# A fused transformer block on one core: a table-load trigger removed, the second feed-forward product and the fusing product in 64-column tiles, its result copied by ScalarE and turned back

## The reference

```python
item, geo, visit = emb[ids], geo_table[ids], visit_table[ids]     # 64, 64, 24 wide
cat   = [gelu(item @ w_item + b), gelu(geo @ w_geo + b), gelu(visit @ w_visit + b)]
fused = layer_norm(gelu(cat @ w_fuse + b_fuse)) * gamma + beta    # exact gelu
h     = item + 0.1 * fused * (ids != 0)
# attention, 4 heads of 16, over 128 tokens of a sequence, on layernorm(h)
h     = h + (softmax(q k^T / 4) v).bf16 @ Wo.T + bo
x3    = layernorm(h)
y     = gelu_tanh(x3 @ w1 + b1) @ w2 + b2                         # 64 -> 256 -> 64
# 63 tokens of each sequence with the largest router weight r = x3 @ wr + br get r * y
out   = h + x3 + where(chosen, r * y, 0)
```

## Time and profile before

| | us |
|---|---|
| median of 3 runs | 574.9 |
| lowest, highest | 573.29, 576.59 |
| the profiled execution, whole | 569.05 |
| its span, first to last instruction | 567.2 |
| PE busy (share of the span) | 463.9 (82%) |
| DVE busy | 434.5 (77%) |
| ACT busy | 376.1 (66%) |
| POOL busy | 344.9 (61%) |
| table loads at L419, L451, L466 | 38.5, 39.8, 41.1 |

### The profile page before, as it was taken

The page is one execution under the profiler, slowest core; times in us unless marked ns, Lnnn a source line. Parts: engine busy times, 40 slices in busy tenths (PEclk is TensorE's granted clock), DMA queues, the critical chain, the costliest instruction groups (busy, mean ns, idle before and its releaser), DMA issues.

```text
span 567.2 us, 16166 instructions
## 1 busy us (share of the span) xinstructions
PE 463.9 (82%) x5636; PEld 362.8 (64%) x5636; DVE 434.5 (77%) x1657; ACT 376.1 (66%) x662; POOL 344.9 (61%) x410
## 2 busy tenths in 40 slices
PE   0677688888899888888888889888888888876853
PEld 0455566666677766676666777776667666665643
DVE  1366677887878878787878888887877887877787
ACT  0425577777777777777777787777777777755540
POOL 5466366765675756666666676666666666431464
PEclk9979899999999999999999999999999999989555
DMA  4112111111110111111111111111111111000244
GB/s 101 22 25 31 15 25 24 24 25 23 17 20 13 20 20 23 23 23 23 23 23 22 20 17 19 17 18 23 23 23 23 23 23 23 1 2 3 70 114 113
DMA packets 23716, 15.80 MB, mean 28 GB/s; under 512 B 18832, under 2 KB 21520, under 8 KB 23568
## 3 DMA queue, kind: packets, MB, share of 16 engines
q0 software_dynamic: 6144, 9.97, 12.3%
q1 hardware_dynamic: 17552, 5.58, 3.7%
HBM read 11.08 MB, written 4.19 MB: 27 GB/s over the span
## 4 chain that ended last, share of the span: by engine, by line
PE 31%; issue 25%; DVE 19%; POOL 11%; ACT 11%; DVEq 1%; DMA 1%; ACTq 0%; POOLq 0%
POOL G L306 5%; ACT prob L466 5%; PE psum L865 4%; PE psum L953 4%; POOL rs L314 4%; PE psum L917 3%; DVE neg_max L614 3%; PE psum L873 3%; PE psum L943 3%; PE psum L810 3%; DVE st L509 3%; PE psum L894 2%; ACT hid L459 2%; DVE mv L516 2%; DVE s L531 2%
## 5 line engine op out<-in xcount | busy, mean ns | idle before, releaser
L314 POOL TENSOR_TENSOR rs<-ve,minus_half 128x4 f32<-128x4 f32 x96 | 101.0, 1052 | 133.3 <-DVE ve L519 128.6
L306 POOL DMA_INDIRECT G<-table,idx x128 | 125.2, 978 | 40.3 <-issue 36.6
L614 DVE TENSOR_REDUCE neg_max<-psum 128x4 f32<-128x512 f32 x128 | 84.4, 682 | 3.9 <-PE psum L865 3.9
L953 PE MATMUL psum<-x3t,wt 64*128 64x256 f32 x256 | 38.3, 420 | 41.9 <-issue 34.9
L459 ACT ACTIVATE hid<-psum,wt 128x512 f32<-128x512 f32 x64 | 40.5, 683 | 45.4 <-PE psum L953 45.4
L786 PE MATMUL psum<-wt,hid 128*128 128x64 f32 x512 | 68.8, 291 | 0.0
L466 ACT ACTIVATE prob<-psum 128x512 f32<-128x512 f32 x128 | 66.1, 603 | 2.0 <-PE psum L828 1.7
L786 PEld LDWEIGHTS psum<-wt,hid 128*128 128x128 f32 x512 | 64.5, 205 | 3.8 <-issue 0.4
L953 PEld LDWEIGHTS psum<-x3t,wt 64*128 64x128 f32 x256 | 23.0, 194 | 50.9 <-issue 41.1
L865 PE MATMUL psum<-k_s,q_s 32*128 32x128 f32 x1024 | 39.3, 292 | 12.5 <-ACT prob L466 12.4
L509 DVE BATCH_NORM_STATS2 st<-psum 128x6 f32<-128x64 f32 x128 | 20.0, 219 | 35.4 <-PE psum L943 30.5
(11 more groups left out here) (113 smaller groups left out, 1084.3 us busy)
## 6 DMA issues: line engine op xcount, KB each, us to landing
out<-R SPq DMA_DIRECT2D x11, 256.0 KB, 2.9
G<-table,idx POOLq DMA_INDIRECT x128
wt<-packed SPq DMA_DIRECT2D x1, 1028.0 KB, 4.9
out<-R SPq DMA_DIRECT2D x2, 512.0 KB, 4.1
q_s<-max_t SPq DMA_DIRECT2D x32, 8.0 KB
out<-R SPq DMA_DIRECT2D x2, 128.0 KB, 2.6
ids_sb<-ids SPq DMA_DIRECT2D x1, 64.0 KB, 1.8
```

Of the source, the lines that this page charges most:

```text
L306: pool.indirect_dma_start(G[par][:, b, :], None, table, bass.IndirectOffsetOnAxis(ap=idx[par][:, b:b + 1], axis=0),).then_inc(gathered[par ...
L314: pool.tensor_tensor(rs[:, :], ve[:, :], minus_half[:, :], ALU.pow).then_inc(S[dst], 1)
L614: dve.tensor_reduce(neg_max[:, GB * h:GB * h + GB], bank[h].rearrange("p (b k) -> p b k", b=GB), AX, ALU.max, negate=True).then_inc(S["max ...
L953: mm(bank[ffn_bank(d) + r][:, m * 2 * P:(m + 1) * 2 * P], w["w_1"][rows, m * P:(m + 1) * P], x3t[rows, :], start=True, stop=True, tile_pos ...
```

## The change

- ACT: the one-element activation (L451) is gone. The x3t copy comes at once after q_s, and the load of the tanh-gelu table stands ahead of the first hid activation.
- PE: the second feed-forward product is turned round. w_2 (64 columns a half) is the stationary side and hid the moving one, four products of 256 columns, two of them at a time in the two column halves of the array. The result comes out with features on partitions, so a new ACT copy (`ffn_copy`, with the bias b_2 added) takes it to SBUF (`y_t`) and two new PE transposes (`ffn_back`) turn it back into PSUM. `ffn_out` on DVE becomes a plain copy. The ACT copy stands between the first and the second exponential, the transposes behind the output projection.
- PE: the fusing product uses one 64-column weight, w_f, in the two column halves for even and odd sequences, in place of two padded weights.
- One weight of 128 columns and the broadcast b2 leave the packed constants.

```diff
-    ("w_ig", P), ("w_vi", 2 * P), ("w_fe", P), ("w_fo", P), ("w_fv", P), ("w_2", 2 * D),
+    ("w_ig", P), ("w_vi", 2 * P), ("w_f", D), ("w_fv", P), ("w_2", 2 * D),
...
+            def ffn_copy(d):
+                wait(act, "f2_ready", 1, d)
+                ends(act, "yb_ready", 1, d - 1)
+                act.activation(y_t[:, :], bank[ffn_bank(d) + 1][:, 0:2 * P], ACT.Identity,
+                               bias=w["b_2"]).then_inc(S["yt_ready"], 1)
...
                 if on(d):
-                    act.activation(loaded[:, :], w["b_q"][0:1, :], ACT.Gelu_apprx_tanh)
                     wait(act, "x3t_ready", 1, d)
                     act.activation(x3t[:, :], bank[ffn_bank(d) + 1][:, 0:2 * P], ACT.Copy
                                    ).then_inc(S["x3t_out"], 1)
+                if type(i) is int and i == NG + 1:
+                    ffn_copy(NG - 2)
...
                                        ACT.Exp, scale=SCALE).then_inc(S["prob_ready"], 1)
+                    if h == 0 and on(d) and not late(i):
+                        ffn_copy(d)
...
             def ffn_out(d):
-                wait(dve, "f2_ready", 1, d)
-                dve.tensor_tensor(
-                    of(Y, d), bank[ffn_bank(d) + 1][:, 0:GB * D].rearrange("p (b d) -> p b d", b=GB),
-                    w["b2"].unsqueeze(1).to_broadcast([P, GB, D]), ALU.add
+                wait(dve, "yb_ready", 1, d)
+                dve.tensor_copy(
+                    of(Y, d), bank[ffn_bank(d) + 1][:, 0:GB * D].rearrange("p (b d) -> p b d", b=GB)
...
             def ffn_second(d):
                 wait(pe, "hid_ready", 2, d)
-                for s in range(GB):
-                    for m in range(2):
-                        last = mm(bank[ffn_bank(d) + 1][:, s * D:(s + 1) * D],
-                                  hid[:, m, slot(s)[0]], w["w_2"][:, m * D:(m + 1) * D],
-                                  start=(m == 0), stop=(m == 1))
+                for m in range(2):
+                    for r in range(2):
+                        last = mm(bank[ffn_bank(d) + 1][r * D:(r + 1) * D, 0:2 * P],
+                                  w["w_2"][:, m * D:(m + 1) * D],
+                                  hid[:, m, r * 2 * P:(r + 1) * 2 * P],
+                                  start=(m == 0), stop=(m == 1), tile_position=(0, r * D))
                 last.then_inc(S["f2_ready"], 1)
+            def ffn_back(d):
+                wait(pe, "yt_ready", 1, d)
+                for j in range(2):
+                    last = mm(bank[ffn_bank(d) + 1][:, j * P:(j + 1) * P],
+                              y_t[:, j * P:(j + 1) * P], ident, start=True, stop=True,
+                              is_transpose=True)
+                last.then_inc(S["yb_ready"], 1)
...
-                    for n, wf in enumerate(("w_fe", "w_fo")):
-                        last = mm(bank[6][:, 0:2 * P], w[wf],
+                    for n in range(2):
+                        last = mm(bank[6][n * D:(n + 1) * D, 0:2 * P], w["w_f"],
                                   cat[:, :].rearrange("p (r s q) -> p s r q", r=2, s=2)[:, n],
-                                  start=False, stop=(n == 1))
+                                  start=False, stop=True, tile_position=(0, n * D))
...
                 if type(i) is int and i == NG + 1:
                     ffn_second(NG - 2)
+                    ffn_back(NG - 2)
...
                 if on(e) and not late(i):
                     project(e)
+                if on(d) and not late(i):
+                    ffn_back(d)
             pipeline(pe, step)
             coefficients(1)
             ffn_second(NG - 1)
+            ffn_back(NG - 1)
```

More of the change, by code:

```diff
@@ L67 @@
     ("w_q", P), ("w_k", P), ("w_v", P), ("w_1", HID),
-    ("w_ig", P), ("w_vi", 2 * P), ("w_fe", P), ("w_fo", P), ("w_fv", P), ("w_2", 2 * D),
+    ("w_ig", P), ("w_vi", 2 * P), ("w_f", D), ("w_fv", P), ("w_2", 2 * D),
     ("w_o", D), ("ident", P),
-    ("gamma", D), ("beta", D), ("bv", D), ("b2", D), ("wr", D), ("br", 1),
-    ("b_ig", 1), ("b_vi", 1), ("b_fu", 1), ("b_q", 1), ("b_k", 1), ("b_1", 2),
+    ("gamma", D), ("beta", D), ("bv", D), ("wr", D), ("br", 1),
+    ("b_ig", 1), ("b_vi", 1), ("b_fu", 1), ("b_q", 1), ("b_k", 1), ("b_1", 2), ("b_2", 1),
 ]
@@ L144, in build @@
         hid = sb("hid", [P, 2, GT])
-        loaded = sb("loaded", [1, 1])
+        y_t = sb("y_t", [P, 2 * P])
         wt_rank = sb("wt_rank", [P, P])
@@ L179, in build @@
             "xw_ready", "w_ready", "r_ready", "x3t_ready", "x3t_out", "f1_ready",
-            "hid_ready", "f2_ready", "y_ready",
+            "hid_ready", "f2_ready", "yt_ready", "yb_ready", "y_ready",
         )}
@@ L468, in step @@
                                        ACT.Exp, scale=SCALE).then_inc(S["prob_ready"], 1)
+                    if h == 0 and on(d) and not late(i):
+                        ffn_copy(d)
             pipeline(act, step)
+            ffn_copy(NG - 1)
         @block.vector
@@ L1009 @@
     wf = np.asarray(L0_tok_w_fuse)
-    c["w_fe"][:, :D] = c["w_fo"][:, D:] = wf[:P]
+    c["w_f"][:] = wf[:P]
     c["w_fv"][:D, :D] = c["w_fv"][D:, D:] = wf[P:]
@@ L1015 @@
     for n, src in (("gamma", L0_tok_ln_gamma), ("beta", L0_tok_ln_beta), ("bv", L0_attn_bv),
-                   ("b2", L0_ffn_b2), ("wr", L0_ffn_wr), ("br", L0_ffn_br)):
+                   ("wr", L0_ffn_wr), ("br", L0_ffn_br)):
         c[n][:] = np.asarray(src).reshape(1, -1)
     c["b_ig"][:D, 0], c["b_ig"][D:, 0] = np.asarray(L0_tok_b_item), np.asarray(L0_tok_b_geo)
-    for n, src in (("b_vi", L0_tok_b_visit), ("b_fu", L0_tok_b_fuse)):
+    for n, src in (("b_vi", L0_tok_b_visit), ("b_fu", L0_tok_b_fuse), ("b_2", L0_ffn_b2)):
         c[n][:D, 0] = c[n][D:, 0] = np.asarray(src)
```

## The result

| | before | changed |
|---|---|---|
| median of 9 runs each, us | 574.7 | 583.8 |
| lowest, highest | 569.49, 576.59 | 576.7, 587.28 |
| the profiled execution | 569.05 | 581.16 |

What follows compares the result with a forecast made beforehand. Two alternating wait loops bound it: ACT/PE (15.25 to 14.2 us: -1.27 + 0.4 - 0.2) and DVE (14.56, then ruling). Saving 0.86 over 26 steps, 22.4 - 2.5 + 0.4, about 20 us off 574.9 gave 555; range 547 to 569.

Steps and rivals of the forecast that it cites:

- The two loops: Waits bounding steps 4 to 29 in turn: one through ACT and PE, 15.25 us a step; one through DVE, 14.56.
- the term for the trigger: ACT in the loop: removing L451 puts the table load under the first feed-forward product; hid starts 1.27 us earlier.
- the written-out steps: Steps 2, 3, 30 and later: table load and first feed-forward product stay sequential; gain 0 to 0.2 us each, taken as 0.
- the first loop: Through ACT and PE, from first feed-forward product via hid and exponentials back: 15.25 us a step before, 14.2 forecast (13.9 to 14.5).
- C: Rival on ACT's table load: it isn't hidden; time within 0.5% of before; chance 0.06.
- The copy: Added ACT copy of y_t between exponentials: costs 0.4 us a step (0.35 to 0.47) on the ACT and PE path, wait 0.
- the product: PE's turned second feed-forward product: 1.0 us instead of 2.00, a gain off the path.
- the tiles: PE's fusing product in two column halves: gain between 0 and 0.5 us a step, taken as 0.2.
- rival D: PE's clock falls within the loop, making the kernel slower; 588 us with four such steps; chance 0.06.
- the phase against POOL: DVE against POOL's fourth gather: short-step phase throughout, so 1.53 us idle before the statistics of fused should go; 2.5 us kept back.
- The 128 x 512 hid halves and all behind them move up by this: ACT's hid and everything after it in the loop start 1.27 us earlier a step.
- Rival A: DVE still meets POOL's gather every second step, 1.17 us more; 15.15 us a step, gain 7, time 568; chance 0.17.

## Why the prediction was wrong, point by point

**The two loops and the term for the trigger: right.** Hid was to start 1.27 us earlier, right behind the product; it is 0.12 behind it on the chips without late starts. In the written-out steps, where the load waits for the product, hid is 1.41 behind it, as forecast. DVE's loop was forecast to take over with 14.56 a step, and it does, with 14.43; the first loop, forecast at 14.2, is nearly as long (14.3). The 20 us forecast are 24 measured there (563 to 539). In the forecast's chances C stood for a load that isn't hidden. No run shows a cost of the load beyond its own 1.28 us: in the changed kernel on chip 4 it runs from 307.57 beside the product (307.60 to 308.74), and hid starts 0.01 us behind it, at 308.86. So C is out.

**The copy, the product and the tiles: about right.** The turned product takes 1.08 us (forecast 1.0) and the copy 0.47 with exponentials around it; alone on the ruling loop it costs 11 us, 0.4 a step over 30 steps (forecast 0.4). The tiles give back 0.3 (forecast 0.2). That all of this would be covered once DVE rules holds to within 1.6 us. PE's busy time fell by less than the 0.8 a step taken in rival D: 13.70 to 13.34 (342.56 and 333.43 over 25 intervals).

**The step that failed: "the phase against POOL".** The prediction said: "If DVE rules in every step, its phase against POOL is that of the short step throughout, so the idle time of 1.53 should go." On the first chip that phase is kept only in part of the steps, and where it is (-0.52 to the gather), DVE's idle time is down to 0.3 in most, but the step isn't short, because something else had moved: the first feed-forward product's end, from +1.95 or +2.44 to +0.64 after the gather's start, from behind the shadow into it. The term "The 128 x 512 hid halves and all behind them move up by this" counted 1.27 us; on the first chip hid starts about 1.9 after the gather whatever the product does. So of 1.27 a large part is taken back: forecast for the ACT and PE loop 14.2, plus the 1.13 by which hid is later than on chip 4 (1.25 - 0.12), is 15.3, and the short steps measure about 15.25. In seven of the 25 steps the statistics fall into the shadow as well (1.8 late), and each such step is about 16.1. Together this takes the whole gain back: without the step of 22.59, and with 0.9 to 1.0 taken off each of the three steps whose clock dipped, the profiled loop has 15.5 a step, where the kernel before has 15.42.

**Rival A had the right suspect and the wrong victims.** It put the stall down to POOL's gather, but priced it as DVE's alone: 1.17 more in every second step, 568 us at most. The row that would have said more was there: hid in the earlier trace rows starts at 311.22, with the fourth gather at 309.19, 2.03 before. Had I asked which other waits would be moved into the time between a gather's start and two microseconds behind it, the answer was hid, by 1.27. I wrote that "one engine's new phase can open other collisions" and gave it no price.

**Rival D came in as a second effect, and most of the loss below the kernel before is with it.** Over the 25 intervals of the two profiled executions the changed kernel is 11.1 us longer (396.63 against 385.56). The one step of 22.59, which has both low clock and late starts in it, is 6.7 us more than the longest of before (15.90), and the three other steps with a dip account for about 3. So the late starts took the gain, and the dips with that one step turned it into a loss. That the dips followed from the late starts is likely (the same kernel has none in its loop on chips 4, 5 and 11, and on chip 14 it has two), but isn't shown. My reason against D, that PE's busy share would stay at 0.89, doesn't decide it either: the share is 342.86 / 396.63 = 0.86 here, and 333.22 / 390.57 = 0.85 in the kernel with only the second product turned round, which has no dip.

**The range.** 547 to 569 holds neither result, 583.8 or 539. It took the kernel's stalls for a matter of 7 us, where they are 12 in the kernel before (575 against 563) and 44 in the changed one (584 against 539.5).

## What to carry to other kernels

When a wait is moved, list what else is under way at its new place, and not only on its own chain: here a stall of 1.5 us in the earlier trace rows, seen and set aside, was the sign of a shadow that the moved wait then fell into in nearly every step. A stall whose cause isn't known is to be priced on every engine that the change moves. Of several edits made at once, time each alone: one line was the whole gain on the chips where there was one, and the rest hid behind the other loop.

## What the runs showed of the hardware

- The kernel before took 563 us on chips 4, 5, 7 and 11 and 575 on chip 14 and the first: 2% between chips. The changed kernel differs by 8%, 539.5 to 584.
- On the latter two chips POOL's indirect DMAs hold back some of the waits of DVE and ACT for PE: in the changed kernel hid, and the statistics that become ready just behind it, started 1.9 to 2.0 us after the fourth gather's start, and around 455 us pv_t came 2.3 us late beside a row of gathers. Other waits beside gathers were served at once (L974 0.05 us behind the end of x3t, 0.13 after the gather's start). On chip 14 ordinary DMAs from the same queue did it in no step of the loop (statistics up to 0.16 behind `fused`, hid 1.25 to 1.27 behind its product's start; 534 us against 571 and 586 with the gathers), and in one of these they stood at the gathers' place. The gather itself takes 0.95 us on either kind of chip (at 312.45 on the first, at 308.10 on chip 4). In the step at 312 us on the first chip ACT is held as long as DVE, to 0.05 us. By what it is held isn't shown.
- A gather's rows are usable 3.4 us after its start, in one place measured.
- With the fourth gather moved, 16 of 25 steps had a stretch at a clock of 0.50 (0.93 over the loop) and took about 1.5 us more than the others; in all the kernel went from 538.4 to 590.4 us. Idle time of PE alone didn't foretell it: 2.29 us a step stood at a clock of 1.00 in the kernel with only the second product turned round, 1.66 a step here.
